# The residual add of an attention epilogue moves from VectorE to GpSimd

## What is computed

```python
def _L0_attn_ref(x, W_qkv, W_out):
    y = jnp.einsum('bsh,oh->bso', x, W_qkv).reshape(*x.shape, 3)
    q, k, v = (y[..., 0], y[..., 1], y[..., 2])
    attn = jax.nn.softmax(jnp.einsum('bqh,bkh->bqk', q, k) * scale, axis=-1)
    return jnp.einsum('bsh,oh->bso', jnp.einsum('bqk,bkh->bqh', attn, v), W_out)
...
x = x + _layernorm(attn(_layernorm(x)))     # attention, one head of width 1024
x = x + _layernorm(ffn(_layernorm(x)))      # gelu FFN 1024 -> 4096 -> 1024,
                                            # times the sum of the router's two top weights
```

## Time and profile before

| | us |
|---|---|
| median of 2 runs | 1833.86 (1821.21 and 1846.51) |
| the profiled execution | 1827.91 |
| span of its slowest core (core 7) | 1826.4 |
| spans of the eight cores | 1796.3 to 1826.4 |
| TensorE busy on core 7 | 1448.6 (79%) |
| VectorE busy | 542.7 (30%) |
| ScalarE busy | 575.7 (32%) |
| GpSimd busy | 132.8 (7%) |

### The profile page before, as it was taken

How to read it: one execution, slowest core, us unless ns; L and a number is a source line. 1 busy time by engine, 2 the same in 40 slices (tenths; PEclk the granted TensorE clock), 3 DMA queues, 4 the chain that set the end, 5 groups by cost and what they waited for, 6 DMA issues and landing times.

```text
span 1826.4 us, 19503 instructions; the slowest of 8 cores (1796.3 to 1826.4 us)
## 1 busy us (share of the span) xinstructions
PE 1448.6 (79%) x6816; PEld 648.2 (35%) x6816; DVE 542.7 (30%) x1054; ACT 575.7 (32%) x1197; POOL 132.8 (7%) x133
## 2 busy tenths in 40 slices
PE   0578787778788888888888888873898898898796
PEld 0233333333333333333333333331343343343342
DVE  0443442554233333333333333333201201201100
ACT  0412121221022333333333333324354354354334
POOL 1000000000000000000000000101013003003003
PEclk9999899998988899898898989886899899899998
DMA  9322112110220010110111111787802002102002
GB/s 137 61 35 46 33 20 41 24 24 1 30 57 7 0 30 29 30 30 29 30 29 30 29 30 29 106 154 137 139 3 96 19 1 84 32 1 88 6 1 81
DMA packets 51616, 81.54 MB, mean 45 GB/s; under 512 B 19648, under 2 KB 27840, under 8 KB 51520
## 3 DMA queue, kind: packets, MB, share of 16 engines
q0 software_dynamic: 27280, 50.35, 16.5%
q1 hardware_dynamic: 24240, 29.94, 5.2%
HBM read 97.08 MB, written 20.97 MB: 65 GB/s over the span
## 4 chain that ended last, share of the span: by engine, by line
PE 68%; DVE 13%; DMA 7%; issue 7%; ACT 4%; POOL 1%; DVEq 0%; SPq 0%; ACTq 0%; POOLq 0%
PE pAll L185 34%; PE pAll L160 30%; DMA xgb<-xo 3%; DVE ptb L750 3%; DMA qs<-qstage 2%; DVE vt L496 2%; PE pAll L216 2%; DVE xfg L439 1%; DVE sm L374 1%; DMA qtile<-qs 1%; DVE m L677 1%; ACT diagb L730 1%; ACT pbuf L688 1%; DVE cfm L789 1%; DMA x2lt<-x2s 1%
## 5 line engine op out<-in xcount | busy, mean ns | idle before, releaser
L160 PE MATMUL pAll<-kf,qtile 128*128 128x512 bf16 x1024 | 258.3, 411 | 18.3 <-DMA qtile<-qs 7.5
L160 PE MATMUL pAll<-x2f,w1b 128*128 128x512 bf16 x1024 | 237.5, 396 | 22.8 <-ACT h1g L1162 18.6
L185 PE MATMUL pAll<-vt,ptb 128*128 128x512 bf16 x1024 | 226.3, 382 | 0.9 <-DVE ptb L750 0.9
L185 PE MATMUL pAll<-w2b,h1g 128*128 128x512 bf16 x1024 | 221.7, 379 | 4.1 <-ACT h1g L1162 4.1
L677 DVE TENSOR_REDUCE m<-pAll 128x1 f32<-128x512 f32 x128 | 88.5, 691 | 337.0 <-PE pAll L160 335.6
L688 ACT ACTIVATE pbuf<-pAll,nb 128x512 bf16<-128x512 f32 x128 | 87.4, 683 | 245.7 <-DVE nb L682 245.7
L160 PEld LDWEIGHTS pAll<-kf,qtile 128*128 128x128 bf16 x1024 | 105.7, 105 | 161.4 <-issue 64.7
L160 PEld LDWEIGHTS pAll<-x2f,w1b 128*128 128x128 bf16 x1024 | 102.9, 101 | 155.1 <-issue 45.6
L185 PEld LDWEIGHTS pAll<-vt,ptb 128*128 128x128 bf16 x1024 | 100.8, 98 | 123.7 <-issue 4.8
L185 PEld LDWEIGHTS pAll<-w2b,h1g 128*128 128x128 bf16 x1024 | 99.9, 98 | 125.9 <-issue 6.0
L185 PE MATMUL pAll<-wvb,xfg 128*128 128x512 bf16 x512 | 115.6, 379 | 35.4 <-DVE vt L496 35.4
(11 more groups left out here) (109 smaller groups left out, 1093.8 us busy)
## 6 DMA issues: line engine op xcount, KB each, us to landing
xrt<-xo POOLq DMA_DIRECT2D x16, 512.0 KB, 5.5
x2s<-x2t SPq DMA_DIRECT2D x16, 512.0 KB, 3.1
w1b<-w POOLq DMA_DIRECT2D x8, 1024.0 KB, 29.6
w2b<-w POOLq DMA_DIRECT2D x4, 2048.0 KB, 43.8
x2rt<-x2s SPq DMA_DIRECT2D x16, 512.0 KB, 4.1
y<-yt SPq DMA_DIRECT2D x16, 512.0 KB, 2.9
xgb<-xo POOLq DMA_DIRECT2D x16, 256.0 KB, 9.0
qs<-qstage POOLq DMA_DIRECT2D x16, 256.0 KB, 3.7
```

Source lines behind the costliest of these rows:

```text
L160: return e.matmul(o(), l(), r(), start=st, stop=sp)
L185: return e.matmul(o(), l(), r(), start=st, stop=sp)
```

## The change

The add of `emit_epi_add` is issued to GpSimd, and counted on `gS`, where it was issued to VectorE and counted on `vS`. Everything that waits for it (`ev_add`) waits for the new event. `ln_stats` gets a parameter that chooses the engine of its sum; no call passes it. A debug branch, not built in the timed kernel, waits for all stores instead of the last.

```diff
     def ln_stats(i, src_fn, sq_fn, stat_waits_v=(), stat_waits_s=(),
-                 src_banks=(), sq_cell=None):
+                 src_banks=(), sq_cell=None, red_eng="vector"):
...
-            ev_red = E.op("vector",
+            ev_red = E.op(red_eng,
                           lambda e: e.reduce_sum(sm, src_fn(), axis=AX),
-                          waits=list(stat_waits_v) + fence, inc="vS")
+                          waits=list(stat_waits_v) + fence,
+                          inc="gS" if red_eng == "gpsimd" else "vS")
...
         wadd = [ev_epi_ln[qt], ev_xrt[qt]]
         if qt - 2 >= 0 and qt - 2 in ev_x2store:
             wadd.append(ev_x2store[qt - 2])
-        ev_a = E.op("vector", lambda e, d=x2a, a=aota, b=xra:
-                    e.tensor_tensor(d, a, b, ALU.add), waits=wadd, inc="vS")
+        ev_a = E.op("gpsimd", lambda e, d=x2a, a=aota, b=xra:
+                    e.tensor_tensor(d, a, b, ALU.add), waits=wadd, inc="gS")
         ev_add[qt] = ev_a
```

More of the change, by code:

```diff
@@ L881, in build_program @@
     if dbg == "B":
-        wlast = [ev_x2store[NQT - 1]] if NQT - 1 in ev_x2store else []
+        wlast = list(ev_x2store.values())
         for t in range(NQT):
```

## The result

| | before | after |
|---|---|---|
| median of the runs, us | 1825.9 (7 runs) | 1801.1 (8 runs) |
| ratio after/before | | 0.986, 95% interval 0.982 to 0.990 |
| profiled execution, us | 1827.91 | 1812.42 |
| slowest core and its span | core 7, 1826.4 | core 1, 1810.9 |
| 13 periods, round 1 to round 14, core 7 | 598.9 | 577.3 |

The time fell by 25 us at the median, to 1801; the forecast was a fall of 21, to 1807.

The account below looks back on a forecast made before the run. TensorE's work plus its gaps bound the kernel. 13 periods of 44.4 us instead of 46.07 gain 21.7 (15.0 add, 6.7 clock and qtile), less 0.8 at the end: 1827.9 - 20.9 = 1807 us, range 1790 to 1830.

Parts of the forecast that it names:

- The add stood ahead of the casts, 13 times 1.15: Gap before the output projection, rounds 2 to 14: removing VectorE's add starts the casts 1.15 us earlier, 15.0 us in all.
- GpSimd's add is hidden: Attention loop: GpSimd's longer add, 2.342 us, is covered by over 25 us of context product and projection.
- Qtile earlier, exp's bank next: Scores: qtile waits of 1.21 us go, exp's bank then costs 0.52; 0.69 us gained in rounds with the qtile wait.
- The clock: Output projections: still slow in most rounds, worst rows vanish; clock and qtile give 6.7 of the 21.7 us gain.
- The sum of 13 periods, 577.2: Core 7, rounds 1 to 14: 13 periods of 44.4 us, where they took 598.9 before, a gain of 21.7.
- The weights of 13 and 3: Of 16 projections behind short gaps in rounds 0 and 1, 13 took about 5.30 us and 3 took 3.61.
- 44.85: Price of a period with a projection of 5.30 us on core 7: 46.00 less 1.15.
- The time: Whole kernel: profiled execution of 1827.9 us less 20.9 makes 1807 us.
- Rival 1, the clock stays up: All 13 projections run at 2.4 GHz, periods 42.41, gain 47.6 less 0.8, 1781 us; chance 0.12.
- Rival 2, all at 6.4: The clock takes the gain: every projection 6.39, periods 46.08, time 1828.8 us; chance 0.10.
- The end of the stage, +0.8: Last add is exposed on GpSimd, so the x2lt loads issue at 1246.8 instead of 1245.95: +0.8 us, once.

Follow-up runs that it names:

- early add on VectorE: Kernel before, add still on VectorE but written right behind the casts of ptb: 1798.5 us against 1825.2, ratio 0.986; a first timing gave 0.990.
- the refilled gap: Kernel after with a 128x1024 filler sum on VectorE in front of the casts of cfm: profiled execution 1816.5 us, another 1826.8, no ratio.
- the add on VectorE, behind the casts: Kernel before, add still on VectorE but written behind the two casts of cfm instead of ahead: ratio 1.017 (0.996 to 1.038).
- a gap of 1.32: Kernel after with VectorE's casts of cfm ahead of the last scores part's max and scaling: 1762.3 us against 1825.2 for the kernel before, ratio 0.967.
- The early sum: Kernel after with the epilogue's sum (VectorE L254) issued during the context product of the round before: profiled execution 1785.9 us, no ratio.
- the half filler: Kernel after with a shorter 128x448 filler sum on VectorE in front of the casts: no ratio, mean period 44.46 to 44.48 on six cores.

## Why the prediction was right, point by point

- **The add stood ahead of the casts, 13 times 1.15.** Right in its cause: the gap is 2.00 in all rounds from 2 to 14. The early add on VectorE and the refilled gap settle it from both sides. The size was a little low: the gap fell by 1.20 in two rounds and by 1.27 in eleven, 16.4 us in all for the 15.0 forecast.
- **GpSimd's add is hidden.** Right: 2.334 us each, and in the round shown over before the context product starts. In round 14, behind the loads of `w1b`, it runs on core 1 from 1182.16 to 1184.51, and ScalarE's copy, which waits for the projection, starts at 1188.50.
- **Qtile earlier, exp's bank next.** Right: no wait for `qtile` inside the loop, 0.52 for the bank. The prediction weighed this at 0.69 in a few rounds, and so undersold it: where the gap was closed and the loads were late (the add on VectorE, behind the casts), the wait came in 12 rounds, 2.0 to 4.0 us each on core 5, and the gain was gone.
- **The clock.** The sum of 13 periods, 577.2, was met by 577.3 on core 7, but that closeness is luck, since two errors cancelled. The weights of 13 and 3 expected some projections of 3.61; rounds 2 to 14 had none. And a period with a projection of 5.30 is 44.4 and not 44.85. The step that failed there is taking one period, 600.25 to 646.25, as the steady price: the first such period after is near it (632.87 - 588.29 = 44.58 on core 7, 44.87 on core 1), and the later ones come down to 44.38 as the second group of scores falls (on core 7 from 5.01 to 4.82). With the weights alone right, the forecast would have been 1812.8, and with the period alone right 1802.
- **The time.** A fall of 20.9 was forecast, and 25 measured at the medians. The forecast priced core 7 alone, and there its 13 periods fell by 21.6. Cores 0 and 1, the longest in these periods, gained 25. That the cores would become alike the forecast did not say; whether this makes up the rest of the 25 is not shown.
- **Rival 1, the clock stays up:** did not come with this change, and did for the projections with a gap of 1.32, at 42.2 a period for the 42.41 priced. The rule of the Trainium skill ("TensorE: Matmul & The Clock Gate", section "Why this matters for your kernels") has the right direction, but it would let a gap of 2.00 pass, and here all 104 projections behind such a gap were slow in the kernel after. A gap of 1.32 kept the clock up in rounds 0 to 14. The early sum shows that a gap of 2.00 can go either way.
- **Rival 2, all at 6.4:** excluded; the gap of 3.1 brings rows of 6.5 back, in every other round. The rival calls such rows the commonest on core 7 before: six of 13 were 6.4 to 6.6, but as many were 4.9 to 5.1.
- **The end of the stage, +0.8.** Too large. Core 1 after, against the earlier trace rows:

```profile
1228.20 1.24 ACT L818 ACTIVATE aot<-aot,nmb,rstd 128x1024 f32<-128x1024 f32 x1
1229.70 2.34 POOL L833 TENSOR_TENSOR x2t<-aot,xrt 128x1024 f32<-128x1024 f32 x1 [6.08 <-ACT aot L818]
1231.98 2.17 POOL L992 DMA_DIRECT2D x2lt<-x2s  x4
```

From the start of ScalarE's last tile to the loads it is 3.78 now and was 3.42: +0.36. The loads follow GpSimd's own add at once, where the prediction had put 0.54 between.

The profiled execution, 1812.4, is above the forecast because core 1 began round 0's projection at 562.1, where it had been at 550.1 before; from there its 13 periods are 24.6 us shorter. The start lies with stage A, which the change doesn't touch; why it was late in this execution is open.

## What to carry to other kernels

Look at what stands ahead of the instruction for which the bounding engine waits, in its engine's queue: an instruction whose inputs were ready long ago belongs earlier, and which engine does it matters less. Follow the queues behind it too, since a store that waits for it can hold loads back, and here closing the gap without moving those gave the gain away. Price a gap of TensorE together with the clock after it: in this kernel half a microsecond between 2.0 and 2.5 was free, and the 0.68 from 2.00 down to 1.32 was worth three times its length.

## What the runs showed of the hardware that was not expected

The loop settles on a period, and the clock after each gap has a part in which one. In the kernel after, at gaps of 2.00, the periods of all cores came down to 44.38, and with the half filler, at 2.5 to 2.9, their mean was 44.46 to 44.48. At 3.1 to 3.3 the loop alternates between about 45.0 and 47.2 for most rounds. At an unchanged gap of 2.00 with the sum early, cores 2 to 7 ran periods near 44.3 and then 40.95 without going back. So the same program with the same gaps has more than one steady period. Why the cores went over when they did stays open.
